# Expert tiles of 128 rows in units of four, and a new order of the pieces

## What is computed

```
x = x + 0.5 * moe(layernorm(x))      # FFN 1
x = x + attention(layernorm(x))      # linear attention, per sequence
x = x + 0.5 * moe(layernorm(x))      # FFN 2, the same weights as FFN 1

moe(x):   scores = sigmoid(x @ router.T)              # 16 experts
          pick 2 of 4 expert groups, then 4 experts of 8 per token
          w = scores of the 4, normalised, times 2.5
          routed = sum over the 4: w * (silu(x@gate.T) * (x@up.T)) @ down.T   # inner size 128
          shared = one dense MLP of inner size 256 over all tokens
          return routed + shared
attention(x): q, k = softplus(gelu(x@w1.T + b1) @ w2.T + b2)   # 16 heads of 16
          v, g = gelu(x@w.T + b)
          z = 1 / (q . sum(k) * scale + 256)
          out = ((q k^T v) * scale + v) * z * g ;  return out @ p_w.T + p_b
```

## Time and profile before

| | |
|---|---|
| median of three runs | 2868.19 us |
| profiled execution: its time / its span | 2862.96 us / 2861.1 us |
| mean granted TensorE clock | 0.802 of 2.4 GHz |
| busy: PE / DVE / ACT / POOL | 65% / 42% / 38% / 39% of the span |
| DMA | 448.61 MB, mean 157 GB/s; the direct queue 42.6% and the indirect one 15.1% of 16 engines' span |
| matmuls | 12,699 |

### The profile page before, as it was taken

One profiled execution on the slowest core, in us unless ns is written; L12 is line 12 of the kernel. 1 busy time (PEld: TensorE's weight loads), 2 busy tenths in 40 slices (PEclk: granted clock), 3 DMA queues, 4 the chain that ended last, 5 costly groups with the idle time before them and its releaser, 6 DMA issues.

```text
span 2861.1 us, 41595 instructions
## 1 busy us (share of the span) xinstructions
PE 1864.8 (65%) x12699; PEld 1338.7 (47%) x12699; DVE 1203.7 (42%) x3475; ACT 1099.0 (38%) x1745; POOL 1121.5 (39%) x1249
## 2 busy tenths in 40 slices
PE   3647566545887458867787777777757675367640
PEld 2325344433665336645564555555535463256430
DVE  3545455434434425434453543445345343242333
ACT  3323333223644226554455345445524431133220
POOL 1455444456022452134233422433351424531456
PEclk7767787767988779978898788889888887789765
DMA  9365675763535786344344544444365458788974
GB/s 340 138 193 155 177 196 157 197 155 122 155 101 123 209 197 141 96 122 129 100 122 129 158 117 116 131 113 129 111 187 132 128 126 227 178 210 213 202 208 132
DMA packets 634972, 448.61 MB, mean 157 GB/s; under 512 B 432760, under 2 KB 591631, under 8 KB 632719
## 3 DMA queue, kind: packets, MB, share of 16 engines
q1 hardware_dynamic: 585426, 311.65, 42.6%
q0 software_dynamic: 49152, 134.28, 15.1%
q10 hardware_dynamic: 188, 0.03, 0.0%
HBM read 135.16 MB, written 243.53 MB: 132 GB/s over the span
## 4 chain that ended last, share of the span: by engine, by line
PE 31%; another core or an unknown queue 22%; issue 16%; ACT 10%; DVE 8%; SPq 8%; POOL 3%; DMA 2%; ACTq 0%; POOLq 0%; DVEq 0%
PE bank L854 4%; PE bank L856 4%; PE bank L855 4%; SPq L835 4%; PE bank L1039 4%; POOL yg L1342 2%; PE bank L996 2%; PE bank L998 2%; PE bank L1100 2%; PE bank L997 2%; ACT ybuf L1200 1%; PE bank L1059 1%; SPq L816 1%; ACT L1193 1%
## 5 line engine op out<-in xcount | busy, mean ns | idle before, releaser
L1328 POOL DMA_INDIRECT xd<-xs,idx x512 | 510.3, 997 | 912.2 <-DVE idx L1476 758.1
L1342 POOL DMA_INDIRECT yg<-yd,idx x512 | 519.7, 1015 | 434.5 <-DVE xb L1554 180.3
L854 PE MATMUL bank<-xtp,gu_hi 128*128 128x256 f16 x1536 | 447.8, 292 | 107.5 <-issue 56.8
L1200 ACT ACTIVATE ybuf<-bank 128x512 f32<-128x512 f32 x384 | 228.6, 595 | 701.6 <-remote 325.8
L996 PE MATMUL bank<-dn_hi,h_hi 128*128 x768 | 230.0, 300 | 402.5 <-ACT ybuf L1200 246.6
L1525 DVE SCALAR_TENSOR_TENSOR sp_g<-bank,sp_g 128x512 f32<-128x512 f32 x256 | 176.8, 690 | 735.9 <-remote 454.4
L855 PE MATMUL bank<-xtp,gu_hi 128*128 128x256 f16 x1536 | 446.8, 291 | 48.1 <-issue 47.3
L856 PE MATMUL bank<-xtp,gu_lo 128*128 128x256 f16 x1536 | 446.7, 291 | 46.6 <-issue 46.3
L1193 ACT ACTIVATE sp_g<-bank 128x512 f32<-128x512 f32 x256 | 152.4, 596 | 409.2 <-remote 210.1
L996 PEld LDWEIGHTS bank<-dn_hi,h_hi 128*128 128x128 f16 x768 | 80.2, 104 | 468.4 <-issue 450.8
L1187 ACT ACTIVATE h_hi<-sp_g 128x512 f16<-128x512 f32 x256 | 159.3, 626 | 249.7 <-DVE sp_g L1525 112.9
(11 more groups left out here) (199 smaller groups left out, 3342.1 us busy)
## 6 DMA issues: line engine op xcount, KB each, us to landing
yd<-ybuf SPq DMA_DIRECT2D x384, 256.0 KB
xd<-zeros SPq DMA_DIRECT2D x128, 256.0 KB
xd<-yg SPq DMA_DIRECT2D x4, 4096.0 KB, 16.0
xr<-xb SPq DMA_DIRECT2D x32, 512.0 KB
xb<-xr SPq DMA_DIRECT2D x32, 512.0 KB
xb<-in_attn_x_dram SPq DMA_DIRECT2D x16, 512.0 KB
xd<-xs,idx POOLq DMA_INDIRECT x512
yg<-yd,idx POOLq DMA_INDIRECT x512
```

Of the source, the lines that this page charges most:

```text
L854: pe.matmul(out_ap, a_hi, b_hi, start=(i == 0), stop=False)
L1200: act.activation(flat(ybuf[:, t % RING_Y]), down_ps[k % DOWNS][:], ACT.Copy).then_inc(yev_done, 1)
L1328: pool.indirect_dma_start(out=xd[q % NC][:, :], out_offset=bass.IndirectOffsetOnAxis(ap=idx[:, r % SEQS, t, k:k + 1], axis=0), in_=xs[:, r ...
L1342: pool.indirect_dma_start(out=yg[:, half, t % 2, j].bitcast(U32), out_offset=None, in_=yd[q % NC][:, :], in_offset=bass.IndirectOffsetOnAx ...
```

## The change

Tiles have 128 rows instead of 256, and a routed unit is four tiles (`quad`) in place of two; it still has 512 columns. The worst case becomes n*512*4 rows plus 127 for each expert, rounded up to whole units: 64, 96, 96 and 64 tiles, 320 for an FFN, 640 in all, which are 160 units. An `xload` issues four transposing DMAs of 128 rows, a unit has four experts and so twice as many gate and up matmuls of half the columns, and each `ystore` issues two DMAs of 128 rows. The zero blocks (`tails`) are four pieces of four DMAs of 128 rows, and `zero_rows` writes half as many rows. `RING_X` goes from 4 to 3 rooms, `RING_Y` from 4 to 5. The scheduler has new costs, and in place of `SETTLE` a single DMA resource that all moves share in turn (`MOVES`), so all engines' orders are laid anew.

```diff
 K2, Q2 = range(2)
 
-SLOT = 256
+SLOT = 128
+QUAD = TOK // SLOT
 ROW = 2 * D
 CHUNKS = (3, 5, 5, 3)
 NC = len(CHUNKS)
-RING_X = 4
+MOST = max(CHUNKS) * TOK // SLOT
+RING_X = 3
 RING_W = 8
 RING_S = 3
 RING_F = 1
 LATE, FILL = 1.5, 1.2
 RING_P = 3
-RING_Y = 4
+RING_Y = 5
 GATES, DOWNS, SIDES = 2, 1, 4
 ROUTE_STEPS = 27
 ROUTED_AT, BASE_AT, IDX_AT = 16, 18, 21
@@ -63,7 +65,7 @@
         first = SEQS * ffn
         for n in CHUNKS:
             tiles = (n * TOK * TOPK + E * (SLOT - 1)) // SLOT
-            tiles += tiles % 2
+            tiles += -tiles % QUAD
             out.append(dict(routings=range(first, first + n), region=n * TOK + SLOT, tile=tile, tiles=tiles))
             first, tile = first + n, tile + tiles
     return out
@@ -75,17 +77,17 @@
 
 
     WEIGHT = dict(
-        SP=dict(wload=0.5, load=0.5, store=0.5, zero_rows=1.0, tails=16.0, xload=3.0, ystore=0.7),
-        PE=dict(turn_w=0.5, small=0.3, turnR=1.0, logits=1.3, rank=0.4, turn_tab=0.3, gate=1.5, up=1.5, down=0.75,
-                turnA=1.8, proj=2.6, second=3.6, gproj=1.3, kv=1.9, z=0.5, apply=1.9, regroup=1.8, out=4.5),
-        ACT=dict(small_hi=1.2, w_hi=0.63, w_copy=0.63, norm=1.8, normA=1.8, xs_hi=1.03, xtf_hi=1.03, xtf_lo=1.03, sigmoid=0.7, silu=0.65,
-                 h_hi=0.63, yev=0.63, xta_hi=1.2, gelu=1.9, absolute=1.05, softplus=6.0, gate_gelu=3.0, ot=2.8),
-        POOL=dict(rootR=0.6, rootA=0.6, scatter=4.1, gather=4.1),
-        DVE=dict(small_lo=0.8, w_lo=0.69, group_p=1.0, stats=2.1, xs_lo=1.25, scores=0.9, groups=2.0, experts=3.2,
-                 slots=2.0, weights=2.2, table_cols=3.5, table=0.3, prod=0.7, h_lo=0.7, shared_sum=0.7, combine=3.7,
-                 statsA=2.1, xta_lo=1.4, add_bias=1.4, gate_bias=0.7, finish=1.25,
-                 kv_mask=0.45, mix=1.6, gate_out=1.9, residual=1.4))
-    SETTLE = dict(wload=3.0, load=3.0, store=3.0, zero_rows=8.0, tails=3.0, xload=3.5, ystore=3.0, scatter=3.0, gather=3.0)
+        SP=dict(wload=0.5, load=0.5, store=0.5, zero_rows=1.0, tails=2.7, xload=2.8, ystore=0.9),
+        PE=dict(turn_w=0.9, small=0.4, turnR=1.2, logits=0.9, rank=0.4, turn_tab=0.5, gate=1.6, up=1.6, down=0.85,
+                turnA=1.2, proj=3.0, second=4.0, gproj=1.6, kv=2.5, z=0.6, apply=2.2, regroup=1.2, out=6.0),
+        ACT=dict(small_hi=0.6, w_hi=0.6, w_copy=0.6, norm=2.1, normA=2.1, xs_hi=1.05, xtf_hi=1.03, xtf_lo=1.03, sigmoid=0.9,
+                 silu=0.62, h_hi=0.63, yev=0.62, xta_hi=1.2, gelu=2.0, absolute=1.05, softplus=5.5, gate_gelu=1.9, ot=3.6),
+        POOL=dict(rootR=1.7, rootA=1.7, scatter=5.1, gather=5.1),
+        DVE=dict(small_lo=0.6, w_lo=0.69, group_p=0.5, stats=1.85, xs_lo=1.25, scores=0.8, groups=1.85, experts=2.3,
+                 slots=1.5, weights=2.2, table_cols=3.7, table=0.3, prod=0.7, h_lo=0.7, shared_sum=0.7, combine=3.3,
+                 statsA=1.85, xta_lo=1.4, add_bias=1.4, gate_bias=0.7, finish=1.25,
+                 kv_mask=0.45, mix=3.0, gate_out=1.45, residual=1.4))
+    MOVES = dict(wload=0.8, load=1.6, store=1.6, zero_rows=7.0, tails=2.0, xload=2.9, ystore=0.85, scatter=1.7, gather=1.7)
     RANK = dict(down=0, silu=0, yev=0, prod=0, rootR=0, rootA=0)
     EARLY = ("stats", "norm", "xs_hi", "xs_lo", "turnR", "xtf_hi", "xtf_lo", "logits", "sigmoid", "scores", "groups",
...
@@ -112,6 +114,7 @@
         self.engine = {name: e for e, pieces in self.WEIGHT.items() for name in pieces}
         self.weight = {name: w for pieces in self.WEIGHT.values() for name, w in pieces.items()}
         self.free = dict.fromkeys(self.WEIGHT, 0.0)
...
@@ -187,7 +190,8 @@
             piece("table_cols", q, ("weights", last))
             piece("turn_tab", q, ("table_cols", q))
             piece("table", q, ("turn_tab", q))
-            piece("tails", q, ("table_cols", q), ("zero_rows", 0))
+            for e in range(0, E, 4):
+                piece("tails", (q, e), ("table_cols", q), ("zero_rows", 0), *[("next", "tails", (q, e - 4))] * (e > 0))
...
         self.span = max(self.free.values())
-        assert not any(self.missing.values()) and len(self.units) == self.pairs + 4 * SEQS
+        assert not any(self.missing.values()) and len(self.units) == self.quads + 4 * SEQS
 
     def put(self, p, at):
         name, key = p
         k = self.order[p] = self.count[name]
         self.count[name] += 1
         self.steps.append(p)
-        end = self.free[self.engine[name]] = at + self.weight[name]
-        landed = end + self.SETTLE.get(name, 0.25)
+        weight = self.weight[name]
+        if name == "down" and self.units[key[0]][0] == "shared":
+            weight *= 2
+        end = self.free[self.engine[name]] = at + weight
+        landed = end + 0.25
+        if name in self.MOVES:
+            self.moved = max(self.moved, at + 0.4) + self.MOVES[name]
+            landed = max(end, self.moved) + 2.0
         if name in self.TAKES:
...
-            return (2 * i, 2 * i + 1)
-
         def tab_of(p, column):
 
-            q = plan.stage_of_tile(2 * p)
-            i = 2 * p - stage[q]["tile"]
-            return tab[0:1, q % NC, column, i:i + 2]
+            q = plan.stage_of_tile(QUAD * p)
+            i = QUAD * p - stage[q]["tile"]
+            return tab[0:1, q % NC, column, i:i + QUAD]
 
         def shared_over(r):
 
             return plan.units.index(("shared", r, 1)) + 1
 
-        unit_of_pair = plan.unit_of_pair
+        unit_of_quad = plan.unit_of_quad
 
         def quarters(n, b):
...
                     sp.wait_ge(consts_ready, CONSTS)
-                    sp.dma_start(zeros[:, :].rearrange("(p j) c -> p (j c)", j=2), block_of_zeros).then_inc(zeros_stored, 16)
+                    sp.dma_start(zeros[:, :], block_of_zeros[:, 0:ROW]).then_inc(zeros_stored, 16)
                 spare = xd[i][E * stage[i]["region"]:rows_of[i], :]
-                sp.dma_start(spare.rearrange("(p b j) c -> p b (j c)", b=E, j=2),
-                             block_of_zeros.unsqueeze(1).broadcast_to([P, E, 2 * ROW])).then_inc(spare_zeroed[i], 16)
-
-            def tails(q):
-
+                sp.dma_start(spare.rearrange("(p b j) c -> p b (j c)", b=E // 2, j=2),
+                             block_of_zeros.unsqueeze(1).broadcast_to([P, E // 2, 2 * ROW])).then_inc(spare_zeroed[i], 16)
+
+            def tails(key):
+
+                q, e = key
                 sp.wait_ge(ends_done, q + 1)
                 if q == 0:
                     sp.wait_ge(zeros_stored, 16)
-                for e in range(0, E, 4):
-                    _, rows4 = nc.values_load_multi_w_load_instructions(
-                        ends[0:1, q, e:e + 4], engines=[mybir.EngineType.SP], min_val=0, max_val=E * stage[q]["region"] - SLOT,
-                        skip_runtime_bounds_check_because="an expert's rows end within its region, a tile before the next one's")
-                    for row in rows4:
-                        sp.dma_start(xd[q % NC][bass.ds(row, SLOT), :], zeros[:, :]).then_inc(tails_filled, 16)
+                _, found = nc.values_load_multi_w_load_instructions(
+                    ends[0:1, q, e:e + 4], engines=[mybir.EngineType.SP], min_val=0, max_val=E * stage[q]["region"] - SLOT,
+                    skip_runtime_bounds_check_because="an expert's rows end within its region, a tile before the next one's")
+                for row in found:
+                    sp.dma_start(xd[q % NC][bass.ds(row, SLOT), :], zeros[:, :]).then_inc(tails_filled, 16)
 
             row_of = {}
 
             def xload(p):
-                q = plan.stage_of_tile(2 * p)
-                if 2 * p == stage[q]["tile"]:
+                q = plan.stage_of_tile(QUAD * p)
+                if QUAD * p == stage[q]["tile"]:
                     sp.wait_ge(tab_done, q + 1)
                     sp.wait_ge(tails_filled, 16 * E * (q + 1))
                     sp.wait_ge(spare_zeroed[q % NC], 16)
                     for i, uses in enumerate(slot_uses(last_route[q], RING_S)):
                         sp.wait_ge(scattered[i], 256 * uses)
                 if p >= RING_P:
-                    sp.wait_ge(up_done, unit_of_pair[p - RING_P] + 1)
-                _, found = nc.values_load_multi_w_load_instructions(
+                    sp.wait_ge(up_done, unit_of_quad[p - RING_P] + 1)
+                _, row_of[p] = nc.values_load_multi_w_load_instructions(
                     tab_of(p, 1), engines=[mybir.EngineType.SP], min_val=0, max_val=rows_of[q] - SLOT,
                     skip_runtime_bounds_check_because="the table holds first rows of whole tiles")
-                for a in range(2):
-                    row_of[2 * p + a] = found[a]
-                    sp.dma_start(xtp[:, p % RING_P, :, a * SLOT:(a + 1) * SLOT], xd[q % NC][bass.ds(found[a], SLOT), :],
+                for a, row in enumerate(row_of[p]):
+                    sp.dma_start(xtp[:, p % RING_P, :, a * SLOT:(a + 1) * SLOT], xd[q % NC][bass.ds(row, SLOT), :],
                                  transpose=True).then_inc(xp_loaded[p % RING_P], 16)
 
```

(33 more changed lines are left out.)

59 lines of the change are left out of this document (29 added, 30 removed).

## The result

The kernel before took 2867.05 us (median of four runs) and the changed one 2916.57 us (2914.13 to 2921.94, four runs): ratio 1.017, 95% interval 1.013 to 1.021. I had forecast 2690 us. The same kernels also ran at a second level, in which the kernel before takes about 2310 us in place of 2790 to 2870; every ratio here is taken within one level, called the upper (2790 and more, the level of the prediction) or the lower.

The account below looks back on a forecast made before the run. No engine was full, so no single bound but four regimes. Gains of 25 (middle), 65 (end), 40, 30 and 15 us (beginning) sum to 175; 2863 - 175 = 2688 profiled, forecast 2690 us, range 2570 to 2880.

Parts of the forecast that it names:

- Bytes and moves: Whole kernel: 58.8 MB fewer of 448.61 MB, 13%, and 320 moves into ybuf, two for each of 160 units.
- the end: 2340 to 2785 us: 53 units become 44, taken as 65 us gained, between 45 and 76.
- DMA sets the pace: In the last stretch, DMA at 0.81 to 0.86 holds units at 8.4 us each; nine fewer save 76 us.
- The group of three: Gate and up on TensorE: three 128-column matmuls cost 0.168 to 0.26 us at the high clock, taken as 0.26.
- PE has slack of a quarter: 1066 to 2340 us: TensorE is busy 74%, so 14 fewer units were taken to gain 25 us.
- the middle: 1066 to 2340 us: 83 units become 69, 25 us gained, bounds 75 gained and 60 lost.
- Rival B: Twice as many register operations pace TensorE in the beginning too, middle loses 60 us; about 2800 us; chance 0.18.
- the beginning: 243 to 1066 us: fewer units gain 40 us up to 504 and 30 to 936, fewer bytes 15 after.
- SyncE's queue: Transposing loads and stores take 4.0 us a unit if priced by rows, 6.5 if per instruction; effect taken as zero.
- The fixed 2 us a transfer: Fixed cost of each DMA besides its bytes, from the Trainium skill; stores' wait longer by some 2 us each ring turn.
- The new order: All engines' orders laid anew: no price in the trace, bounded at 60 us either way in the middle, taken as zero.
- C: Three rooms: sequences' stay sets attentions' period, about 2940 us; sign: periods above 105 us, load behind each store; chance 0.13.

Follow-up runs that it names:

- e9: Kernel before with each routed gate and up matmul of 256 columns split into two of 128, each with a weight load; 2902.08 us, ratio 1.038, upper level.
- e11: Kernel before with TensorE's expert numbers fixed when it is written, so register operations are left out; 2739.69 us, ratio 0.981 to the kernel before, upper level.
- e8: Changed kernel with four rooms, ybuf ring of four, four transposing loads priced at 5.8 us, not 2.8; 2159.36 us, 0.935 to the kernel before, lower level.
- e4: Kernel before, four rooms and 256-row tiles kept, its order laid with the new costs and shared transfer resource; 2211.44 us, ratio 0.956, lower level.
- e16: Changed kernel with four rooms for rows and four for results; 2864.66 us, ratio 1.000 to the kernel before, upper level.
- e5: Changed kernel, unedited, run again at the lower level; 2160.99 us, ratio 0.938 to the kernel before.
- e17: Kernel before with the new durations in the planner alone, its own tiles and units kept; 2801.57 us, ratio 0.976 to the kernel before, upper level.

## Why the prediction was wrong, point by point

**Bytes and moves right, the end right by luck.** 58.2 MB for 58.8, and 320 moves. The end gave 67 us, where I had put 65. But mine were 9 units fewer at the old pace, and what came were 22 fewer at a worse one, 11.1 us for 8.3, with DMA at 0.61, so "DMA sets the pace" did not hold. I had also read ACT's waits of rows 6 as the store of ybuf. All 12 of them, the 71.8 us, ended with the semaphore of TensorE's `down`; where a store was waited for as well, it had landed 2.9 us before or more. A ybuf ring of 5 has little to relieve there.

**The group of three: right where it was read, wrong as a bound.** Weight loads of after:

```profile
1970.37 0.10 PEld L860 LDWEIGHTS bank<-xtp,gu_hi 128*128 x1 [0.49 <-issue]
...
1970.61 0.10 PEld L860 LDWEIGHTS bank<-xtp,gu_hi 128*128 x1
...
1970.84 0.10 PEld L860 LDWEIGHTS bank<-xtp,gu_hi 128*128 x1
```

Groups start 0.24 us apart here. I counted 588 groups at 0.22 to 0.24 us and 817 at 0.15 to 0.18: both ends of my bound occur. But the upper end was not 0.26 us. In the stretches it is 5.6 us, and the trace of before had shown it, at 1708 us: "issue" between matmuls of one group. **This is the step that failed.** I wrote "PE has slack of a quarter", bounded the loss of the middle at 60 us, and put the price of more instructions at nothing beyond 0.26 us a group. Part of that idle quarter was not slack: at the upper level every instruction added costs 11 to 14 ns (e9, e11), and the change adds 7,808, 89 to 105 us. Rival B had the right engine and the wrong price (0.26 us a group, 110 us in all); its sign, a granted clock below 0.75 in the middle, did not come (0.80).

**The middle and the beginning.** I had 25 us and 85 us gained and got 49 and 70 lost, in windows cut a little differently; the beginning is the largest miss of all the terms. The forecast of the beginning also took it that fewer units start the attentions earlier; the new order puts more units first, 39 for 30.5, and does so at the lower level too, where the first `apply` moves from 544 to 580 us and the middle gives it back (1317 us to 1171).

**SyncE's queue.** The duration of each instruction, min/median/max in ns:

```profile
L840 SPq DMA_TRANSPOSE xtp<-xd x640: 4/1189/2796, 144.7 to 2758.3; - x160
```

The price is per instruction, 1.19 us for 128 rows against 1.25 for 256: my upper bound, 6.5 us a unit. Pricing it in the planner brings under 1% at the lower level (e8), where SyncE is the second largest share of the chain; that only shows that the planner need not know it, and what it costs at the upper level, with the pauses on top, was not measured. The fixed 2 us a transfer that the prediction takes from the Trainium skill (DMA: Bandwidth & Descriptors, Anatomy of one DMA) are given there for transfers that POOL issues, and these stores are issued by SyncE; no run here shows such a share.

**The new order: taken as zero, worth 4.4% at the lower level and 2.4% at the upper.** It is the largest gain in the whole change, and the one that I called unpriced. My 60 us of bound, for the middle alone, were too few: e4 gained 101.

**Three rooms.** The signature of C came, with the stay of 307 us shown above, but the rooms explain about 65 us (27 to 52 us by the medians, 2892 and 2917 to 2865, between chips). A fourth room lengthens the stays, to 388 us in e16 (load at 1306, store at 1694): the period fell by 6.7 us, not to 307 / 4. At the lower level the stay is 222 us (e5: load, then store; the time between is left out), so the limit is 74 us where the period is 78:

```profile
965.49 0.38 SPq L790 DMA_DIRECT2D xb<-xr  x1
...
1187.74 0.58 SPq L800 DMA_DIRECT2D xr<-xb  x1
```

**The agreement at the lower level is no confirmation.** 2690 / 2867 is 0.938, and e5 gave 0.938. But there the tiles brought 1% in the old order and 2.3% in the new one (2211 to 2161 us), where I had them at 6%, and the order 4 to 5%, where I had zero. Two errors cancelled.

The version to keep is e17, the kernel before with the new durations: faster than both at the upper level (0.976), and than the kernel before at the lower (0.957). Where the lower level can be counted on, the changed kernel is better (0.938). No kernel here beats both kernels at both levels.

## What to carry to other kernels

Before idle time of an engine is called slack, look at what ended it. "Issue" between instructions that wait for nothing is a sign of a price per instruction, and a change that splits the same work into more instructions may pay it again, as e9 did. Look for it in the timeline of the second and third instruction of a group, where no data can be late. Before an unnamed releaser is given a name, read in the kernel what the waiting instruction waits for: if no transfer is among it, it was none. A planner's durations are an edit of their own; run them alone, since they can be worth more than the change that they come with.
